# The gelu's odd low halves move from GpSimd to VectorE, in a graph network kernel on one core

## What is computed

```python
h = relu(layernorm(x))
for l in range(3):                       # "L0": three layers of attention and feed-forward
    scores = leaky_relu(h @ a_i + (h @ a_j).T + b)         # masked by the adjacency
    h1 = layernorm(h + softmax(scores) @ h) * g1 + beta1
    h  = layernorm(h1 + gelu(h1 @ W1 + b1) @ W2 + b2) * g2 + beta2   # W1 256x1024, W2 1024x256
x = x + h
h = relu(layernorm(x))                   # "L1": one graph attention layer (GAT)
x = x + elu(softmax(masked leaky_relu scores of h @ W) @ (h @ W))
```

## Time and profile before

| | |
|---|---|
| median of three runs | 2628.86 us |
| the profiled execution | 2635.33 us |
| its span, first to last instruction | 2633.6 us |
| TensorE busy | 2320.5 us, 88% |
| VectorE busy | 1848.1 us, 70% |
| ScalarE busy | 1579.8 us, 60% |
| GpSimd busy | 1271.1 us, 48% |
| mean granted TensorE clock | 0.973 |

### The profile page before, as it was taken

The page is one execution under the profiler, slowest core; times in us unless marked ns, Lnnn a source line. Parts: engine busy times, 40 slices in busy tenths (PEclk is TensorE's granted clock), DMA queues, the critical chain, the costliest instruction groups (busy, mean ns, idle before and its releaser), DMA issues.

```text
span 2633.6 us, 41679 instructions
## 1 busy us (share of the span) xinstructions
PE 2320.5 (88%) x14721; PEld 1733.9 (66%) x14721; DVE 1848.1 (70%) x4914; ACT 1579.8 (60%) x2426; POOL 1271.1 (48%) x2199
## 2 busy tenths in 40 slices
PE   4888999988899988998989989899878899999968
PEld 4566666766666666776766757667666677666646
DVE  8476678548777686776876868767757676666755
ACT  4366565645666575565766566656637566656544
POOL 3345455644275344663455542745526455545511
PEclk9899999999999999999999999999989999999988
DMA  6212021101220112110211101301131010100000
GB/s 209 103 41 85 6 74 55 57 1 48 73 73 5 37 57 80 57 41 1 89 53 53 41 32 58 101 5 41 41 96 53 5 41 9 37 9 21 23 12 31
DMA packets 66222, 128.57 MB, mean 49 GB/s; under 512 B 12985, under 2 KB 53213, under 8 KB 62942
## 3 DMA queue, kind: packets, MB, share of 16 engines
q1 hardware_dynamic: 66014, 125.90, 14.2%
HBM read 111.20 MB, written 14.68 MB: 48 GB/s over the span
## 4 chain that ended last, share of the span: by engine, by line
PE 55%; DVE 24%; issue 8%; ACT 8%; POOL 6%; DMA 1%; DVEq 0%; SPq 0%; POOLq 0%; ACTq 0%
PE OB L1484 36%; PE FB L1484 12%; DVE pw L1133 5%; DVE mj L1109 3%; PE RB L1484 3%; ACT nms L816 3%; DVE junk L1049 3%; DVE st L998 2%; PE TH L1484 2%; DVE gT L1147 2%; DVE xc L1025 1%; DVE junk L1054 1%; ACT gT L793 1%; POOL rs L581 1%; PE TH L1525 1%
## 5 line engine op out<-in xcount | busy, mean ns | idle before, releaser
L1484 PE MATMUL OB<-xx,pw 128*128 128x257 f32 x4096 | 960.0, 389 | 22.2 <-DVE xc L1025 13.1
L1484 PEld LDWEIGHTS OB<-xx,pw 128*128 128x128 f32 x4096 | 771.4, 193 | 163.4 <-DVE xc L1025 19.6
L1484 PE MATMUL FB<-hT,wb 128*128 128x512 f16 x2304 | 568.5, 385 | 73.9 <-DVE gT L1147 57.3
L1484 PE MATMUL OB<-wb,gT 128*128 128x256 f16 x4608 | 574.1, 275 | 27.6 <-DVE xc L1025 18.1
L1484 PEld LDWEIGHTS OB<-wb,gT 128*128 128x128 f16 x4608 | 450.4, 99 | 168.3 <-DVE xc L1025 23.1
L612 POOL TENSOR_TENSOR gT<-g,gT 128x512 f16<-128x512 f32 x192 | 227.8, 1187 | 418.4 <-ACT gT L793 417.1
L1484 PEld LDWEIGHTS FB<-hT,wb 128*128 128x128 f16 x2304 | 213.0, 99 | 289.4 <-DVE gT L1147 67.5
L799 ACT ACTIVATE pw<-pw,sj 128x512 f32<-128x512 f32 x512 | 334.0, 711 | 57.5 <-DVE pw L1133 57.0
L757 ACT ACTIVATE xc<-xc,nb,rs 128x256 f32<-128x256 f32 x384 | 212.6, 590 | 234.0 <-POOL nb L584 233.9
L576 POOL TENSOR_SCALAR ve<-mv 128x2 f32<-128x2 f32 x256 | 60.0, 234 | 606.5 <-DVE mv L1001 594.2
L1133 DVE SCALAR_TENSOR_TENSOR pw<-r2s,sj,RB 128x512 f32<-128x512 f32 x446 | 315.7, 738 | 43.7 <-PE RB L1484 43.0
(11 more groups left out here) (118 smaller groups left out, 2644.6 us busy)
## 6 DMA issues: line engine op xcount, KB each, us to landing
wb<-w_scratch SPq DMA_DIRECT2D x19, 2048.0 KB, 7.9
adjst<-in_adj SPq DMA_DIRECT2D x56, 512.0 KB, 4.3
xx<-in_x SPq DMA_DIRECT2D x16, 512.0 KB, 5.5
nm<-in_L_gnn_W SPq DMA_DIRECT2D x6, 1024.0 KB, 8.6
gb<-in_L_gnn_g SPq DMA_DIRECT2D x48, 128.0 KB, 2.8
adjst<-in_x SPq DMA_DIRECT2D x6, 1024.0 KB, 11.1
out_x<-adjst SPq DMA_DIRECT2D x48, 128.0 KB, 1.7
pw<-in_adj SPq DMA_DIRECT2D x4, 1024.0 KB, 9.9
```

Source lines behind the costliest of these rows:

```text
L1484: return pe.matmul(o, lhsT, rhs, start=first, stop=last)
```

## The change

All sixteen low halves of a step are made by VectorE from the PSUM bank. The gelu is always written back into `FB`. GpSimd's `g_low` and the buffer `g32` are gone, and with them ScalarE's wait for the previous odd low half. `hidden(n + 2)` with n odd now waits for the low half of n (`glo_odd`) and no longer for the gelu.

```diff
-        g32 = sb("g32", [P, HALF])
...
-            def g_low(k, n):
-                i = NF * fi(k) + n
-                pool.wait_ge(ghi_done, i + 1)
-                pool.tensor_tensor(out=gT[:, i % GRING, 1, :], in0=g32[:, :], in1=gT[:, i % GRING, 0, :],
-                                   op=ALU.subtract).then_inc(glo_odd, 1)
...
                 for n in range(NF):
-                    if n % 2 == 1:
-                        g_low(k, n)
                     if n == 11:
...
                 src = FB[i % 2][:, :]
-                if n % 2 == 1:
-                    if i >= 2:
-                        act.wait_ge(glo_odd, i // 2)
-                    dst = g32[:, :]
-                else:
-                    dst = src
-                act.activation(dst, src, ACT.Gelu, bias=b1c[:, layer(k), f:f + 1], scale=1.0 / W_SCALE)\
+                act.activation(src, src, ACT.Gelu, bias=b1c[:, layer(k), f:f + 1], scale=1.0 / W_SCALE)\
                    .then_inc(gelu_done, 1)
...
-                act.activation(gT[:, i % GRING, 0, :], dst, ACT.Copy).then_inc(ghi_done, 1)
+                act.activation(gT[:, i % GRING, 0, :], src, ACT.Copy).then_inc(ghi_done, 1)
...
                 dve.tensor_tensor(out=gT[:, i % GRING, 1, :], in0=FB[i % 2][:, :], in1=gT[:, i % GRING, 0, :],
-                                  op=ALU.subtract).then_inc(glo_even, 1)
+                                  op=ALU.subtract).then_inc(glo_odd if n % 2 else glo_even, 1)
...
                 for n in range(NF):
-                    if n % 2 == 0:
-                        g_low(k, n)
+                    g_low(k, n)
...
                 if i >= 2:
-                    if i % 2 == 0:
-                        pe.wait_ge(glo_even, i // 2)
-                    else:
-                        pe.wait_ge(gelu_done, i - 1)
+                    pe.wait_ge(glo_odd if i % 2 else glo_even, i // 2)
```

## The result

The changed kernel takes 2608.98 us (median of 4 runs, 2607.15 to 2610.01), the kernel before beside it 2631.0 (4 runs, 2627.74 to 2633.87): a ratio of 0.9916 [0.9899, 0.9933], 22 us or 0.8% faster. The forecast was 2621, 8 us faster. The profiled executions have spans of 2606.9 and 2633.6 us, 26.7 apart, at the same mean granted clock of 0.973.

The account below looks back on a forecast made before the run. TensorE (busy 2320.5 of 2633.6 us) was the bound; terms +9.5, -11.2, -6.0, -3 and +2.7 gave -8.0 on 2635.33, so 2627.3, less 6.5 for execution against median: 2621. Range 2603 to 2658, the forecast's own 2611 to 2632.

Parts of the forecast that it names:

- early gain: Without GpSimd's low halves its means and scales come earlier, so gelus start sooner: -11.2 us in raw, -6.0 in GAT-side steps.
- plain loss: Five steps without extra work (1, 2, 25, 26, 27): 1.6 us at the head plus 0.3 in the tail, +9.5 together.
- nine others: Ahead steps 9, 13, 17, 21 and steps 0, 3, 4, 5, 23: 0.3 us each from an exposed low half, +2.7.
- Removed instructions, raw steps: Steps 7, 11, 15, 19, carrying the next graph's masks and first norm: earlier scales save 2.8 us each, -11.2.
- GAT side: Steps 8, 12, 16, 20, 24, 28: GAT norm's earlier scales halve a 1.28 us wait; 1.0 us each, -6.0.
- Added instructions: VectorE's 192 new low halves: 684 ns each, 131.3 us; free where it waits anyway, 0.6 us where it has no gap.
- Added wait at the plain head: Head of a plain step: an odd tile's first product waits for VectorE's low half, 1.6 us (bounds 1.0 to 2.3).
- Tails: From tile 8 in raw and GAT-side steps: 2.6 us in, 3.1 back; -0.3 each, ten steps -3; plain +0.3.
- Rival A: VectorE's order becomes the bound: reductions stay stretched and each tail pays, +25.5 us, 2654 us; chance 0.25.
- Rival C: The early gain is larger: step 3 and GAT-side steps gain like the raw ones, 2611 us; chance 0.17.
- The signs: VectorE busy up about 90 us, ScalarE's nb wait down 20 or more, gT wait some 75, plain +1.9, raw -3.

Follow-up runs that it names:

- e10_order: Kernel before, all GpSimd low halves kept; in raw and GAT-side steps GpSimd makes means and scales ahead of low halves and affine work: 2601.97 us, ratio 0.9884.
- e5_sbuf: Changed kernel, odd gelus written to the SBUF buffer again, VectorE's low half made from there, odd tile's first product waiting for the gelu alone: 2632.17 us.
- e6_early1: Changed kernel with VectorE's low half 1 placed directly behind low half 0: 2610.35 us, ratio 0.9907.
- e8_late: Kernel before with only odd tiles 9, 11, 13 and 15 of a step moved to VectorE: 2630.54 us, ratio 0.999.
- e1_same: Changed kernel with GpSimd still stopping for each odd gelu copy, then doing a same-shape subtraction whose result is unused: 2699.51 us, ratio 1.025.
- e12_both: Kernel before with scales first (except step 3) and odd low halves split between GpSimd and VectorE by kind of step: 2584.06 us, ratio 0.981.

## Why the prediction was right, and where it was not

The direction, the mechanism of the early gain and the size of the plain loss were right. The size of the whole was not: the forecast gain of 8 us is about a third of what came (22 between the medians, 26.7 between the spans). The time lies in the stated range (2603 to 2658) but 2 us outside the forecast's own (2611 to 2632). Of the 18.7 us between -8 and -26.7, 11.7 lie in the nine others, 4.2 in step 1, 2.5 in the plain steps and 2.4 in raw and GAT-side ones, less 1.8 in the GAT steps.

The largest single part of the miss is a term that the forecast did not have, the place of TensorE's stretches at half clock. TensorE works at half clock for 103.9 us before and 103.8 after. But 13.7 us of this work have moved into the GAT steps 10, 14, 18 and 22, which are only 0.3 us longer for it in all. In the other steps there is as much less. By an estimate (last section) that is worth 6.9 us of the 26.7 in all, and 11.6 of the 15.9 us that the nine others and step 1 miss the forecast by. That part of the gain is luck, as far as the forecast goes.

- **Removed instructions, raw steps.** Right at every station of the walk (above) and in size: -13.8 for four steps where -12.4 was forecast. The cause is shown by e10_order: with the scales first, the same steps gain 12.0 with all low halves still on GpSimd.
- **GAT side.** -8.8, forecast -7.8. The wait before the first GAT product of step 20 fell from 1.28 us to 0.26, about the 1.0 that I took. What I missed is that far more was to be had: the order alone gives 18.5 there. The diagonal edges of VectorE that I thought would eat the gain are not what holds these steps.
- **Added instructions.** 684 ns and 131 us right. VectorE's busy time rose by 48, not 90: the reductions gave back 50.3 us over the whole kernel, where I had counted tails alone, and other instructions 33.
- **Added wait at the plain head.** +5.1 for four steps with their tails, forecast +7.6. The size held (+1.2 us a step for 1.6); the reason did not. I let the place of low half 1 between the row maxima decide; e5_sbuf and e6_early1 took that wait away for nothing. It is the amount of VectorE's work there, two low halves of 0.6 us. Step 1, which I had counted as plain, gained 2.3, of which 1.7 is clock by the same estimate.
- **Tails.** Right as a sum (e8_late: ratio 0.999), wrong in its parts: 2.0 us back in a raw tail and not 3.1. By the rule of the Trainium skill that the prediction weighed, the relief would have been whole; by proportion 2.0. The trace gives 2.0, but GpSimd's other work also slid under the reductions, so it does not refute the rule.
- **The nine others.** The term that was furthest off: +2.7 forecast, -9.0 measured (-3.9 ahead, -5.1 the rest). TensorE works at half clock for 63.8 us in these steps before and for 44.0 after, which is worth 9.9 us, more than all that they gained. Without it they come to +0.9. Ahead step 9, at the full clock in both, shows what the change itself does: it is 0.4 us longer. Its wait for a score unit behind tile 4 fell from 2.47 to 1.68 us, but a new one of 1.03 for a low half stands ahead of it, and the wait behind its tail rose from 1.23 to 2.87.
- **Rival A** is wrong: with the late low halves alone (e8_late) a raw step is 0.3 us longer, where it had 2.6, and ahead step 9 0.2, where it had 1.3. But e1_same shows what it was afraid of: the same VectorE work beside a GpSimd that goes on as before costs 66 us.
- **Rival C** (2611) is nearest to the time, but not for its reason. It wanted step 3 and the GAT-side steps to gain like the raw ones. A raw step gained 3.5, a GAT-side one 1.5 and step 3 1.9, and of the wait of 1.69 us 0.69 is left. (It also counted five such steps where there are seven.)
- **The signs** came out: ScalarE's waits for nb fell by 49 us (20 or more), TensorE's for VectorE's gT rose to 71.5 (some 75), a plain step is 1.3 us longer (1.9) and a raw one 3.5 shorter (3).

What stays open: what decides where the stretches at half clock fall; how the 66 us of e1_same divide between VectorE's order, traffic and the clock (TensorE works at half clock for 43 us more in it than before, worth 21); and how much of e10_order's gain on the GAT side is owed to the scales coming before the low half and how much to their coming before the affine work, since it moved them ahead of both.

## What to carry to other kernels

An in-order engine with spare time can still be the one that everybody waits for. Before moving work off it, look at what it makes that others wait for, and put that ahead of what stops for a late input: here four lines of order brought more than moving 192 instructions. When an engine has a stretch without a gap, an added instruction costs its length there, and a better place for it only moves the wait. And test the change by halves (which tiles, which steps): here one half brought the whole 24 us and the other nothing clear of the spread, and the best version was a mix.

## What the hardware did that I had not expected

TensorE's granted clock took part in the result, by its place and not by its sum. It has two levels in these traces, the full 2.4 GHz and the half. A 128x512 product follows the one before it by 0.22 us at the full clock and by 0.43 at the half. So the time in which TensorE works at the half clock, divided by two, is what the clock costs it, as an estimate (the stretches are read from the trace, by the two values of the granted clock).

In ahead step 13 of the kernel before, a stretch of 10 us was granted 0.83 on average; in ahead step 9, at the same place in the step, none of it was at the half clock (windows of the kernel before):

```profile
1216.00:1226.00 10.00, 7.29 (x51) 4.57 (x50) 4.26 (x7) 4.98 (x8) 4.01 (x6) 0.83 0.01 2
903.70:913.70 10.00, 7.27 (x58) 4.74 (x57) 5.58 (x9) 5.03 (x8) 4.06 (x6) 1.00 0.00 0
```

TensorE had done the same in both: it stood 2.47 us for a score unit (this row is of step 13; in step 9 the same wait ends at 908.33).

```profile
1220.58 0.42 PE L1484 MATMUL RB<-identb,nms 128*128 128x128 bf16 x4 [2.47 <-DVE pw L1133]
```

Steps 13, 17 and 21 of before are 92.0 to 92.2 us long, step 9 is 90.5. In the changed kernel all four are 90.7 to 90.9 and at the full clock. There a stretch of 3.4 us at half clock stands 0.8 us behind the start of the GAT step instead, right after the wait of 2.87 us. Step 10 of before and of the changed kernel:

```profile
948.12:982.62 34.50, 31.79 (x176) 26.66 (x177) 31.34 (x100) 29.46 (x49) 14.40 (x24) 1.00 0.21 80
```

```profile
937.79:972.43 34.64, 32.95 (x176) 27.95 (x177) 31.38 (x100) 28.59 (x47) 14.17 (x23) 0.95 0.17 69
```

TensorE is busy 1.2 us longer and the step is not: here the slower products fill time in which it would have waited. Summed by steps, the work at half clock is

```
                 steps 10, 14, 18, 22   nine others   step 1   GAT side   6, 29, 30   all
before                     0.0              63.8        6.8       0.0        30.6     103.9
changed                   13.7              44.0        3.4       3.4        36.8     103.8
```

(raw and last steps are under 2.1 each). Outside the first column it is 13.8 us less, worth 6.9.

It is no rule that fewer waits keep the clock up in a given step. In e12_both step 13 is granted 1.00 and step 17, with equal waits, 0.97, and is 1.7 us longer (windows of their feed-forward parts):

```profile
1182.70:1236.00 53.30, 46.25 (x361) 31.50 (x361) 35.67 (x71) 31.27 (x47) 20.39 (x34) 1.00 0.04 10
1487.50:1542.00 54.50, 47.91 (x361) 32.08 (x361) 35.28 (x71) 30.85 (x46) 20.37 (x34) 0.97 0.04 9
```

GAT step 29 goes the other way: 25.4 us of waits before and 25.0 after, and 2.2 us longer after the change, its middle granted 0.77 where before was granted 0.86. I cannot say what decides where such a stretch falls. The length of one step should be compared only with its granted clock beside it.

The second surprise is the price of 1.1 us of GpSimd's time: 22 us for 192 pieces that move almost nothing (8 of it in longer busy time of TensorE), on an engine that is busy 40% of the time.
